# Image pairs moved between HBM and SBUF in whole rows of 64 columns instead of two halves of 32

## What is computed

```python
x = x + conv3x3_mean(ln_over_channels(x))      # depthwise, every tap 1/9, zero padding
t = to_tokens(x)                               # one token of 256 channels per pixel
n = ln_over_channels(t)
#   per token: three 16-way argmax(n[...] > 0.5) over channels 16..63 give nibbles,
#   channels 0..2 give the masks, channels 65 and 66 two flags;
#   two 3-layer MLPs of width 80 (weights Wa, Ws) run on these features
f = n
f[64:80] += 2 * one_hot(res_lo);  f[72:88] += 2 * one_hot(res_hi);  f[80] += carry
x = from_tokens(t + f)
```

## Time and profile before

| | |
|---|---|
| median of 3 runs | 781.53 us (779.17 to 781.85) |
| the profiled execution | 780.83 us, of which the span from the first to the last instruction is 779.0 us |
| VectorE busy | 651.8 us, 84% of the span |
| TensorE, ScalarE, GpSimd busy | 67%, 63%, 57% |
| mean granted TensorE clock | 0.928 |
| packets of the DMA queue q1 | 625984, 67.46 MB |

### The profile page before, as it was taken

One profiled execution on the slowest core, in us unless ns is written; L12 is line 12 of the kernel. 1 busy time (PEld: TensorE's weight loads), 2 busy tenths in 40 slices (PEclk: granted clock), 3 DMA queues, 4 the chain that ended last, 5 costly groups with the idle time before them and its releaser, 6 DMA issues.

```text
span 779.0 us, 10762 instructions
## 1 busy us (share of the span) xinstructions
PE 524.5 (67%) x2258; PEld 237.7 (31%) x2295; DVE 651.8 (84%) x1479; ACT 487.7 (63%) x739; POOL 444.4 (57%) x708
## 2 busy tenths in 40 slices
PE   0044567877777777768777777777777777789660
PEld 0011223333323333333333333333333333334320
DVE  1729988999999999959999999969999999997540
ACT  0101577777666677757667677657776677779930
POOL 0203766676677666646677666636667766666400
PEclk9976799999999999989999999989999999999995
DMA  9599991297069907793069907750129009557999
GB/s 106 48 134 192 198 182 23 37 164 126 14 96 146 179 1 109 94 172 61 12 97 149 174 0 108 98 66 0 27 29 161 1 0 105 31 59 51 81 86 77
DMA packets 626042, 68.02 MB, mean 87 GB/s; under 512 B 625856, under 2 KB 625984, under 8 KB 625984
## 3 DMA queue, kind: packets, MB, share of 16 engines
q1 hardware_dynamic: 625984, 67.46, 73.6%
HBM read 33.90 MB, written 33.55 MB: 87 GB/s over the span
## 4 chain that ended last, share of the span: by engine, by line
PE 21%; DVE 20%; issue 19%; ACT 15%; DVEq 1%; ACTq 1%
ACT xbuf L800 10%; DVE n L556 8%; PE ps L840 8%; PE ps L879 4%; DVE stat L565 3%; ACT h L770 3%; DVE xbuf L583 2%; ACT h1m L762 2%; PE ps L890 2%; PE ps L882 2%; DVE yy L505 2%; DVE ycar L509 2%; PE ps L877 2%; PE ps L898 1%; PE ps L906 1%
## 5 line engine op out<-in xcount | busy, mean ns | idle before, releaser
L556 DVE TENSOR_SCALAR n<-xbuf,mean,rn 128x256 f32 (+1 forms) x256 | 234.8, 952 | 0.0
L800 ACT ACTIVATE xbuf<-xbuf,shift,gain (+1 forms) x256 | 223.2, 942 | 0.0
L672 POOL TENSOR_TENSOR nlo<-n,nhi 128x1024 f16<-128x1024 f32 x64 | 145.5, 2274 | 131.5 <-ACT nhi L783 131.5
L783 ACT ACTIVATE nhi<-n 128x1024 f16<-128x1024 f32 x64 | 67.7, 1057 | 214.9 <-DVE n L556 214.9
L565 DVE BATCH_NORM_STATS2 stat<-xbuf 128x6 f32 (+1 forms) x256 | 173.6, 682 | 19.5 <-DMA xbuf<-x 19.5
L840 PE MATMUL ps<-nhi,band 128*128 128x512 f16 (+1 forms) x408 | 117.5, 406 | 24.3 <-DVE xbuf L583 12.5
L879 PE MATMUL ps<-h1m,w2m 128*128 128x512 f32 x256 | 130.7, 592 | 0.0
L681 POOL TENSOR_TENSOR ut<-xbuf,mean 128x536 f32<-128x536 f32 x32 | 44.4, 1388 | 136.9 <-DVE shift L485 136.9
L583 DVE TENSOR_TENSOR xbuf<-ps,xbuf 128x512 f32 (+1 forms) x128 | 90.8, 709 | 37.2 <-PE ps L840 22.0
L840 PE MATMUL ps<-nlo,band 128*128 128x512 f16 (+1 forms) x408 | 113.0, 393 | 0.0
L882 PE MATMUL ps<-h1lo,w2r 128*128 128x512 f32 x128 | 55.4, 433 | 75.3 <-DVE h1lo L597 75.3
(11 more groups left out here) (94 smaller groups left out, 732.4 us busy)
## 6 DMA issues: line engine op xcount, KB each, us to landing
xbuf<-x SPq DMA_DIRECT2D x16, 1024.0 KB, 11.5
out<-xbuf SPq DMA_DIRECT2D x32, 512.0 KB, 7.1
xbuf<-x SPq DMA_DIRECT2D x30, 512.0 KB, 7.2
out<-xbuf SPq DMA_DIRECT2D x12, 1024.0 KB, 12.7
out<-xbuf SPq DMA_DIRECT2D x16, 256.0 KB, 8.2
xbuf<-x SPq DMA_DIRECT2D x4, 256.0 KB, 6.5
consts<-cst SPq DMA_DIRECT2D x1, 170.0 KB, 2.4
h<-ws SPq DMA_DIRECT2D x8, 10.0 KB
```

Of the source, the lines that this page charges most:

```text
L556: ins = v.tensor_scalar(n32[:, w // HALF, w % HALF, :], xview(par)[:, jc * CW + w, :], mean[:, k, w:w + 1], rn[:, k, w:w + 1], ALU.subtrac ...
L672: pool.tensor_tensor(nlo[:, at:at + HALF, :], n32[:, h, :, :], nhi[:, at:at + HALF, :], ALU.subtract).then_inc(lo_ready, 1)
L783: act.activation(nhi[:, at:at + HALF, :], n32[:, s, :, :], ACT.Copy).then_inc(hi_ready, 1)
L800: ins = act.activation(col, col, ACT.Identity, bias=shift[:, k, w:w + 1], scale=gain[:, k, w:w + 1])
```

## The change

```diff
 GROUPS = CW // 2
-HALVES = 2
+HALVES = 1
 HALF_W = W // HALVES
```

## The result

The changed kernel takes 797.52 us in the median of 4 runs (795.97 to 798.11), the kernel before 780.72 (779.17 to 781.85). The ratio is 1.0213, 95% interval 1.0188 to 1.0239: 2.1% slower. The forecast was 790.3 with a range up to 794.0; the direction was right, the size not. The profiled execution has a span of 796.2 us, 17.2 more than before.

What follows compares the result with a forecast made beforehand. The prediction took VectorE's own work as the bound, with transfers counting only where somebody waits. 780.83 + 11.1 (wait of step 2) - 2.3 (branch back) = 789.6 us profiled, 790.3 as the median; range 784.5 to 794.

Steps and rivals of the forecast that it cites:

- What bounds the kernel: Whole kernel: VectorE, busy 84% of the span; after the start no engine of the computation waits for a transfer.
- three places to look at: Where DMA time can count: the wait of step 2, the loop's branches back, and the tail.
- The wait of step 2: VectorE waiting for pair 0's columns from 16 on: now awaited whole, 6.29 MB, a delay of 11.1 us passed on in full.
- I take the ceiling: First load of pair 0: 218 GB/s taken as a ceiling in bytes, 28.9 us plus 2.4 lost between transfers.
- The bounds: Time of the first load in 192-byte runs: 21.6 us at least, 26.4 between, 31.3 at most.
- the upper one at 31.3 us: First load of pair 0: 6.29 MB at 218 GB/s with 2.4 us lost between transfers, a delay of 11.1 us.
- the rival in which width is free: First load: only the number of runs counts, delay 1.4 us, time 780.6 us; chance 0.06.
- The rival of a slow first load: First load of pair 0 at 174 GB/s, below the ceiling: delay 18 us, time 797 us; chance 0.06.
- The branch back: Steps 15 and 23: with no xbuf traffic the first stall falls from 8.07 to 5.74 us, a gain of 2.3 us.
- the second stall: VectorE idle 5.74 us at 518.88 behind the second branch back, taken as what the first stall would fall to.
- The reloads: Storing pair 0 and loading pair 2 before step 16, and the second reload: in time with 6 to 15 us slack, cost nothing.
- The rest: Pair 1's load, the tail and the wait dropped from steps 4, 12, 20 and 28: no effect on the time.

Runs made afterwards that it cites:

- e2_start_only: Kernel before with only pair 0's columns 16 to 63 loaded in one piece of 192-byte runs, all else in halves: 801.54 us against 780.04, ratio 1.0279.
- p2_sides: Kernel before with sixteen groups of isolated transfers ahead, varying HBM and SBUF start, run length, 64 or 128 partitions, loads and stores: 128-byte loads at 217 and 218 GB/s.
- p1_runs: Kernel before with nine isolated loads of different column ranges put ahead, one at a time over 64 partitions: 9.4 to 20.0 ns a run.
- e3_quiet_short: Kernel before with the first half of each pair stored and reloaded two chunks later, runs still short: 775.27 us against 780.04, ratio 0.9938.
- e7_one_more: Changed kernel with one more instruction in VectorE's written-out part ahead of the loop (a memset split in two): 797.77 us, ratio 1.0220 to the kernel before.
- e1_split_start: Changed kernel with pair 0's columns 16 to 63 again in two pieces, all else in whole rows: 775.95 us against 780.04, ratio 0.9951.

## Why the prediction was wrong

**What bounds the kernel** was read rightly. The queue's busy share bought nothing, and there were three places to look at.

**The wait of step 2** is where it failed, in the sentence "I take the ceiling". The term was 11.1 us and measured 21.4. The mechanism around it was right: the wait is at the place given, delays all that follows in full (e2_start_only: + 21.5 us for this edit alone), and later steps take as long as before. The size was wrong because the row of 128 bytes was read as a ceiling in bytes. Its 218 GB/s is the price of one piece of 128 bytes, 9.4 ns (p2_sides has the same 218 over twice the partitions), and a run of 192 bytes has two, 19.9 ns. The first load ran at 154 GB/s. The bounds were wrong too. All of them, the upper one at 31.3 us included, drew smooth lines through 64 and 128 bytes, and the price is a staircase. Two equal times for 64 and 128 bytes were in front of me; I used them for the rival in which width is free, and did not ask what else gives equal times below a width and not above it. The rival of a slow first load, at 174 GB/s and 797 us, had the time right by luck: 174 is the rate on which stores of 128-byte runs settle in p2_sides, and none of the loads of p1_runs settles on it.

**The branch back**: direction right, size low. 2.3 us came from the second stall as the quiet one; the changed kernel's are 3.9 and 4.3 us, those of e3_quiet_short 4.7 and 5.3. e3_quiet_short shows 3.9 us less idle time and 4.8 us less time for quiet queues alone. In the changed kernel the idle time falls by 5.6, of which 1.7 goes with the place of the code and, by e7_one_more, not with the time. The prediction also named the traffic wrongly: what is under way behind the first branch before is stores of pair 1's first half (the 174 GB/s) and then loads of pair 3's, not pair 2's. For the gain this made no difference.

**The reloads** cost nothing, as said, with 16 us of slack instead of 6 to 15. **The rest**: no effect, as said.

Mended, the sum is 780.7 + 21.4 - 4.1 (e1_split_start) = 798.0, against 797.5 measured. The 21.4 is this kernel's own wait; e2_start_only, which has the slow load alone, gives 21.5.

## What to carry to other kernels

Ask of every longer run who waits for its transfer: here 230 thousand packets fewer were worth nothing, since outside the start no engine waited for one, while joining a piece needed early to one needed late cost 21 us. For loads in runs of up to 256 bytes, count pieces of 128 bytes as SBUF's addresses cut them, not bytes or runs: a run within one piece is best filled to 128 bytes, and one of 128 bytes must not straddle a boundary. And look at what moves behind a loop's branch back: shifting the stores and reloads of the first halves away from it gave 4.8 us.

## What was not expected of the hardware

- Once settled, a load from HBM over 64 partitions of 64, 128, 160, 192 or 256 bytes a run takes an engine 9.4, 9.4, 20.0, 19.9 and 20.0 ns a run when SBUF's side starts on 128 bytes, and 128 bytes that straddle in SBUF take 18.8. The Trainium skill (DMA: Bandwidth & Descriptors, "How a descriptor splits into AXI transactions") puts the boundary at 256 bytes of the descriptor's address. Here columns 0 to 31 and 32 to 63 start 128 bytes apart, so that one of them is off such a boundary, and both load at the full 218 GB/s: the measurement decides.
- Stores of one piece settle lower than loads. Columns 0 to 31 (172.4 to 184.3 us of p2_sides) go from 218 to 174 GB/s, 11.8 ns a run, and whole rows (229.4 to 250.3 us) stay at 205; both rows stand below. Columns 16 to 47 are stored at 109; whether SBUF's boundary or HBM's counts there was not tested.

```profile
GB/s 139 215 217 218 218 216 190 173 175 174 173 175 175 173 175 174 173 174 175 173 175 175 173 174 176 172 175 175 173 174 174 173 175 173 174 173 175 175 173 66
...
GB/s 148 204 204 206 205 205 204 204 206 204 199 205 204 206 205 204 207 204 204 205 204 206 205 203 208 204 204 205 205 199 204 204 205 205 205 205 205 204 205 108
```

- Behind a branch back of this loop VectorE stands idle for 3.9 to 5.3 us with no transfer of `xbuf` under way, and for 8.1 with stores and loads under way. That it waits for instructions is read from the packets of their queue at those places; the runs show only that transfers lengthen the wait.
